# A batch's recurrence beside the whole next iteration, its feed-forward one iteration later, with three x buffers

## The chip, the cores and the metric

The program runs on one core of a Trainium2 chip. The metric is the device time of one execution in microseconds (us). Of the kernel before there are three timed executions: 1560.98, 1566.29 and 1566.89 us, median 1566.29. One more execution was profiled; it took 1569.24 us, of which 1567.4 us lie between the first and the last instruction (its span).

## What is computed

The reference is one decoder layer on x of 16 batches, 256 tokens and 512 channels, each of three parts followed by a residual and a layer norm:

```python
x = _layernorm(x + _L0_attn_ref(x, Wq, bq, Wk, bk, Wv, bv, Wo, bo))      # causal attention, 16 heads of 32
x = _layernorm(x + _L0_xattn_ref(16, 256, 512, time_decay, time_first, x, ctx_2048))
x = _layernorm(x + _L0_ffn_ref(x, W_gate, W_qkv))
```

The second part is a recurrence over the 256 tokens, per channel, with key x and value ctx:

```python
ww = u + kt;  q = max(pp, ww);  e1 = exp(pp - q);  e2 = exp(ww - q)
y_t = (e1 * aa + e2 * vt) / (e1 * bb + e2)
ww2 = pp + w; q2 = max(ww2, kt); e1b = exp(ww2 - q2); e2b = exp(kt - q2)
carry = (e1b * aa + e2b * vt, e1b * bb + e2b, q2)
```

The third part is again causal attention with 16 query heads, but with one key and one value head for all of them: a gate (softmax of x @ W_gate.T, then its argmax) picks for each token one of 16 key and value heads.

## The kernel before, in words

The 16 batches are independent. The names A, W and F stand for the three parts of a batch: first attention, recurrence, feed-forward attention. Every float32 matrix product is made of three f32r products (high x high, low x high, high x low), so that each operand is split once: ScalarE (ACT) writes the high part from PSUM, VectorE (DVE) the rest. In the code these are the functions ending in `_hi` and `_lo`.

Heads are handled in four groups of four. For a group, TensorE (PE) computes the scores twice. `sq` (three tiles) gives them with queries on partitions; DVE reduces each tile to a negated maximum (L1368); PE transposes those (`max_transpose`, L547); ACT and DVE split the row in two, `row_hi` and `rows` (L1373); two DMAs on SyncE (SP) write the rows into `q_stack`. Then `sk` (three tiles) computes the scores with keys on partitions, now with the maxima included; ACT takes the exponential (L1031); PE multiplies with the values (`values`), ACT copies, PE turns back (`turn`), DVE normalises. The operands `q_stack` and `k_stack` are built by DMAs out of `q_hi`, `q_lo`, `k_hi`, `k_lo` (`stack`, L322). In A, `out_transpose`, `out_hi` and `out_lo` prepare the output projection (jobs PA_WO and PA_WO + 1); `first_residual`, `first_stats` and `ln_apply` follow.

The recurrence works on the transposed x: `x1_transpose` brings a half (two blocks of 128 channels) into a PSUM bank. For each of the four blocks c DVE runs `recurrence_start` (a scan for the maxima and a difference), ACT five activations in `carry_exps` and one in `now_exps`, GpSimd (POOL) `weighted`, DVE `sums` (two scans), POOL `products`, DVE `divide` (a reciprocal), POOL `quotient`. `y_transpose` brings a half back, then `second_residual`, `second_stats`, `second_norm`. F starts with `x2_transpose`, projections on jobs PF_Q, PF_K, PF_V (two each), `gate_logits`, `gate_transpose`, `gating`, `pick_key`, `key_transpose`, `pick_value`, and then has the same four groups.

There is no scheduler. Each engine's order is written by hand, and semaphores join them. The steady part is `iteration(t)`: it runs A of batch t (from its last value projection on), F of batch t - 1, and at its end the first projections of batch t + 1 and the recurrence of batch t. The recurrence of t starts when A of t is through its layer norm and must end before F of t can start, early in the next iteration. `opening` runs batch 0 alone, `ending` the last recurrence and the last F. x of a batch stays in one of two buffers, `x_even` and `x_odd`. Eight PSUM banks exist: `pp` and `pw` for projections and transposes, `pt` for small transposes, two for `sq`, two for `sk`, `po`. All projections of the next batch go through `pp` from batch 2 on. Each engine works its list strictly in order: an instruction that waits holds all behind it.

## Time and profile before

| | us |
|---|---|
| median of three timed executions | 1566.29 |
| the profiled execution | 1569.24 |
| its span | 1567.4 |
| busy in the span: PE, DVE, ACT, POOL | 1419.3, 1124.4, 640.0, 412.3 |
| first and last x split for the next batch on ACT (L1102, 15 of them) | 61.7 and 1370.5 |

The profile gives the work of each engine over the span. PE is busy 91% of it, DVE 72%, ACT 41% and POOL 26%. In the chain of work that ended last PE holds 59% and DVE 26%. Busy time is a sum over parts of the program with different limits, so it has to be read by stretch. The ends of matmuls in the profile are modelled, since matmuls overlap; an idle time of PE is therefore shown shorter than the gap that it makes between the starts of two matmuls.

### The profile page before, as it was taken

The page shows a single profiled execution, that of the slowest core. Times are in us where ns is not written, and L with a number is a line of the kernel's source. Part 1 is how long each engine was busy: PE and PEld are TensorE (multiplying, and loading weights), DVE is VectorE, ACT ScalarE, POOL GpSimd, SP SyncE. Part 2 cuts the span into 40 slices and gives each one's busy share as a digit, 9 for nine tenths or more (in the row PEclk, how much of TensorE's full clock was granted, in tenths as well). Part 3 has the DMA queues.
Part 4 walks back from the last instruction along what each step waited for, and adds up shares of the span by engine and source line. Part 5 has one row for each costly group of instructions (what it writes and reads, how often), then busy time and mean ns, then how long its engine had stood idle before and what let it go on. Part 6 is the DMA issues. An engine that isn't in the chain of part 4 may idle for free.

```text
span 1567.4 us, 26626 instructions
## 1 busy us (share of the span) xinstructions
PE 1419.3 (91%) x9941; PEld 1123.7 (72%) x9941; DVE 1124.4 (72%) x2260; ACT 640.0 (41%) x1459; POOL 412.3 (26%) x550
## 2 busy tenths in 40 slices
PE   7879999899998989999899999989999998999886
PEld 6667777677777777777777777777777777777564
DVE  4475777868677686776868677786867768677774
ACT  3442533434344253433435344353434425353322
POOL 1350321414122141321414122141412214032130
PEclk9989999999999999999999999999999999999998
DMA  6432232333213233232333313233321323323110
GB/s 192 133 89 68 55 76 57 88 89 79 79 42 82 75 88 89 59 88 52 71 88 79 92 47 74 65 88 89 79 79 42 82 75 89 88 61 80 32 50 20
DMA packets 63199, 119.50 MB, mean 76 GB/s; under 512 B 14304, under 2 KB 32736, under 8 KB 63072
## 3 DMA queue, kind: packets, MB, share of 16 engines
q1 hardware_dynamic: 60400, 112.56, 28.6%
q10 hardware_dynamic: 2672, 5.24, 1.0%
q8 instruction: 80, 1.31, 0.4%
q14 instruction: 47, 0.39, 0.1%
HBM read 32.81 MB, written 8.39 MB: 26 GB/s over the span
## 4 chain that ended last, share of the span: by engine, by line
PE 59%; DVE 26%; ACT 7%; DMA 3%; issue 3%; SPq 1%; POOL 1%; DVEq 0%; ACTq 0%; POOLq 0%
PE pp L485 8%; PE pp L487 7%; PE pp L486 7%; PE po L590 7%; DVE neg_max L1368 5%; DVE w_key L1445 3%; PE po L594 3%; PE sq L531 3%; DVE w_max L1439 2%; PE sq L525 2%; PE pw L485 2%; PE pw L487 2%; PE pw L486 2%; PE sq L510 2%; DMA q_stack<-max_rows 2%
## 5 line engine op out<-in xcount | busy, mean ns | idle before, releaser
L1031 ACT ACTIVATE prob<-sk 128x512 f32<-128x512 f32 x384 | 215.0, 594 | 464.2 <-PE sk L510 463.7
L1368 DVE TENSOR_REDUCE neg_max<-sq 128x2 f32<-128x512 f32 (+1 forms) x384 | 249.7, 677 | 58.0 <-PE sq L510 54.9
L485 PE MATMUL pp<-xt_hi,w_hi 128*128 128x256 f32 x728 | 220.4, 303 | 20.8 <-DVE w_lo L1355 7.3
L487 PE MATMUL pp<-xt_hi,w_lo 128*128 128x256 f32 x728 | 206.3, 283 | 0.0
L486 PE MATMUL pp<-xt_lo,w_hi 128*128 128x256 f32 x728 | 206.3, 283 | 0.0
L485 PEld LDWEIGHTS pp<-xt_hi,w_hi 128*128 128x128 f32 x728 | 139.8, 192 | 32.9 <-issue 11.8
L486 PEld LDWEIGHTS pp<-xt_lo,w_hi 128*128 128x128 f32 x728 | 139.9, 192 | 0.7
L487 PEld LDWEIGHTS pp<-xt_hi,w_lo 128*128 128x128 f32 x728 | 139.6, 192 | 0.0
L1042 ACT ACTIVATE o_ch<-po 128x512 f32<-128x512 f32 x128 | 75.8, 592 | 136.2 <-PE po L594 136.2
L510 PE MATMUL sq<-mask_qk,ident_b 128*128 128x256 bf16 (+1 forms) x384 | 124.7, 325 | 0.0
L485 PE MATMUL pp<-w_hi,xt_hi 128*128 128x512 f32 x252 | 114.2, 453 | 10.7 <-DVE k_lo L1477 10.7
L510 PE MATMUL sk<-mask_kq,ident_b 128*128 128x256 bf16 (+1 forms) x384 | 123.4, 321 | 0.0
L1854 POOL TENSOR_TENSOR w_ev<-w_e,w_val 128x256 f32<-128x256 f32 x62 | 43.6, 704 | 260.8 <-ACT w_e L1089 229.0
L1445 DVE RECIPROCAL w_key<-w_key 128x256 f32<-128x256 f32 x62 | 107.5, 1734 | 0.0
L1820 POOL TENSOR_TENSOR var_eps<-meanvar,eps 128x2 f32<-128x2 f32 x48 | 9.3, 194 | 359.6 <-DVE meanvar L1404 359.6
L487 PE MATMUL pp<-w_hi,xt_lo 128*128 128x512 f32 x252 | 99.6, 395 | 0.0
L486 PE MATMUL pp<-w_lo,xt_hi 128*128 128x512 f32 x252 | 98.9, 392 | 0.0
L563 PE MATMUL sk<-q_stack,kf_stack 98*128 98x512 f32 x192 | 82.1, 467 | 6.9 <-DMA q_stack<-max_rows 3.3
L1373 DVE TENSOR_TENSOR max_rows<-pt,max_rows 8x128 fp32r<-8x128 f32 x128 | 35.3, 276 | 72.5 <-ACT max_rows L1064 70.0
L1839 POOL TENSOR_TENSOR xt_lo<-x_raw,xt_hi 128x1024 fp32r<-128x1024 f32 x15 | 35.6, 2373 | 189.9 <-ACT xt_hi L1102 189.9
L590 PE MATMUL po<-prob,v_f 128*33 128x256 f32 x512 | 80.0, 388 | 3.5 <-ACT prob L1031 2.3
L590 PE MATMUL po<-prob,v_a 128*33 128x256 f32 x512 | 80.7, 393 | 1.1 <-ACT prob L1031 1.1
(237 smaller groups left out, 3537.1 us busy)
## 6 DMA issues: line engine op xcount, KB each, us to landing
q_stack<-q_hi SPq DMA_DIRECT2D x256, 128.0 KB, 2.4
q_stack<-q_lo SPq DMA_DIRECT2D x128, 128.0 KB, 2.4
k_stack<-k_hi SPq DMA_DIRECT2D x128, 128.0 KB, 2.3
x_raw<-in_xT SPq DMA_DIRECT2D x16, 512.0 KB, 3.8
k_stack<-k_lo SPq DMA_DIRECT2D x64, 128.0 KB, 2.3
w_val<-in_ctxT SPq DMA_DIRECT2D x62, 128.0 KB, 2.2
w_raw<-in_weights ACTq DMA_DIRECT2D x4, 1024.0 KB, 6.5
q_stack<-max_rows SPq DMA_DIRECT2D x256, 4.0 KB
```

Of the source, the lines that this page charges most:

```text
L485: T.matmul(out, lh, rh, start=(c == 0), stop=False, skip_group_check=True)
L486: T.matmul(out, lh, rl, start=False, stop=False, skip_group_check=True)
L487: mm = T.matmul(out, ll, rh, start=False, stop=(c == CC - 1), skip_group_check=True)
L510: return T.matmul(out, ident_b[:], tile[:].unsqueeze(1).to_broadcast([P, heads, P]), start=False, stop=True, skip_group_check=True)
L531: T.matmul(out[:, S * k:S * (k + 1)], q_stack[0:3 * HD, h, P:S], key(h, 0, S, 3 * HD), start=(k == 0), stop=False, skip_group_check=True)
L563: T.matmul(out[:].rearrange("p (h q) -> p h q", h=heads), key(h, lo, P, rows), q_stack[0:rows, h:h + heads, q], start=True, stop=False, sk ...
L590: T.matmul(po[VW * j:VW * j + HD + 1, at:at + S], value(0, HG * g + k), prob0[:, k, :], start=True, stop=False, skip_group_check=True)
L594: mm = T.matmul(po[VW * j:VW * j + HD + 1, at + P:at + S], value(1, HG * g + k), prob1[:, k, :], start=False, stop=True, skip_group_check= ...
L1031: A.activation(dst, sk[n % 2][:], ACT.Exp, scale=SCALE).then_inc(s_exp, 1)
L1042: A.activation(o_ch[:].rearrange("p h q -> p (h q)"), po[:], ACT.Copy).then_inc(s_och, 1)
L1368: V.tensor_reduce(dst, src, AX.X, ALU.max, negate=True).then_inc(s_max, 1)
L1445: V.reciprocal(key, key).then_inc(w_rec, 1)
```

## The change

An iteration t now runs A of batch t, the second half of the recurrence of batch t - 1 (blocks 2 and 3), and F of batch t - 2; at its end stand the first half of the recurrence of batch t and the projections of t + 1. So three batches are under way, and x has three buffers. Iteration 1 has no F. `ending` has the rest of F of batch 13, all of F of batch 14, the last recurrence and F of batch 15. The overlays of recurrence buffers on `k_stack`, `k_hi` and `k_lo`, the second set of recurrence buffers for the last batch (`far`) and POOL's rewriting of the rows of ones in `k_stack` (`ones_back`) are gone. `picked` has a buffer of its own. The projections PA_K and PA_V of the next batch go to `pw`, so that Q, Q + 1, K, K + 1, V alternate as pp, pp, pw, pp, pw. The `keep` fillers of the ending are gone. All five engines' lists are rewritten.

```diff
-        k_stack, far_max, far_e2, far_d, far_e1, far_key, w_key, w_e1 = overlaid(
...
+        k_stack = sb("k_stack", [P, NH, S], f32r)
+        w_key = sb("w_key", [P, HC, S])
+        w_e1 = sb("w_e1", [P, HC, S])
...
-        x_even = sb("x_even", [P, TT, D])
-        x_odd = sb("x_odd", [P, TT, D])
+        x_bufs = [sb(f"x{i}", [P, TT, D]) for i in range(3)]
...
         def bank_of(b, job):
...
-            return pp
+            return pw if job in (PA_K, PA_V) else pp
...
+            def x1_transpose(b, half):
                 pe.wait_ge(x1_ready, b + 1)
+                wait(pe, w_free, W_JOBS * b + W_X1J + half)
+                if half == 1 and b == LAST:
+                    pe.wait_ge(u_free, U_JOBS * (b - 1) + U_X2 + 1)
+                elif half == 1 and b:
+                    pe.wait_ge(pa_free, PA_JOBS * (b + 1) + PA_V + 1)
+                turn_half(pw, x_of(b), half).then_inc(w_job, 1)
...
+            def x2_transpose(b):
                 pe.wait_ge(x2_ready, b + 1)
+                if b < LAST - 1:
+                    pe.wait_ge(w_free, W_JOBS * (b + 1) + W_X1J + 2)
...
-                        wait(pe, pf_free, PF_JOBS * b)
+                        wait(pe, pf_free, PF_JOBS * (b - 1))
...
                     elif job < PA_WO:
-                        wait(pe, pa_free, PA_JOBS * b + job)
+                        pe.wait_ge(pa_free, PA_JOBS * b + job - 1)
+                        if job == PA_K:
+                            pe.wait_ge(w_free, W_JOBS * (b - 1) + W_X1J + 1)
...
+            def iteration(t, last=False):
+                r, b = t - 1, t - 2
+                f = b >= 0
...
+                project_a(t, PA_V + 1, {1: lambda: sq_a(t, 0, 2), 2: first_max})
+                sq_a(t, 1, 0, 1)
+                if f:
+                    x2_transpose(b)
+                sq_a(t, 1, 2)
...
+                sk_a(t, 0, 0, 1)
+                max_a(t, 1)
+                sk_a(t, 0, 2)
...
+                if f:
+                    project_f(b, PF_V, fourth_turn)
...
+                    project_f(b, PF_V + 1, lambda: sq_f(b, 0, 2))
+                    max_f(b, 0, a_free, A_JOBS * a_done)
+                    sq_f(b, 1, 0, 1)
                 project_a(t, PA_WO)
...
             def iteration(t, last=False):          # on DVE
+                if t > 1:
+                    recurrence_start(r, 2)
+                maxima_a(t, 0, 2)
+                if t > 1:
+                    recurrence_start(r, 3)
+                rows_a(t, 0)
+                if b >= 1:
+                    last_third_residual(b - 1, x_of(b - 1))
+                maxima_a(t, 1, 0, 1)
+                if f:
+                    x2_split_lo(b, 0)
+                    x2_split_lo(b, 1)
                 maxima_a(t, 1, 2)
...
-            def ones_back(b):
...
             opening()
-            iteration(1, 1)
-            for t in range(2, NB - 1):
-                iteration(t, t % 2)
-            iteration(NB - 1, 1, True)
+            for t in range(1, NB):
+                iteration(t, t == LAST)
             ending()
```

How the change moves work is seen in two places. The first is DVE at the head of a steady iteration. Before, behind the first two maxima of group 0 of A (`neg_max`), there stand the sums of blocks 2 and 3 of the previous batch (L1437, L1439), its reciprocals (`w_key`) and its first residual (`x_odd<-pw`):

```order
L1368 TENSOR_REDUCE neg_max<-sq1 128x2
L1437 SCALAR_TENSOR_TENSOR w_e2<-w_e1_58,w_e2 128x256
L1439 SCALAR_TENSOR_TENSOR w_max<-w_e1_58,w_ev 128x256
L1368 TENSOR_REDUCE neg_max<-sq0 128x2
L1437 SCALAR_TENSOR_TENSOR w_e2<-w_e1_58,w_e2 128x256
L1439 SCALAR_TENSOR_TENSOR w_max<-w_e1_58,w_ev 128x256
L1373 TENSOR_TENSOR max_rows<-pt,max_rows 8x128
L1445 RECIPROCAL w_key_57<-w_key_57 128x256
L1368 TENSOR_REDUCE neg_max<-sq1 128x4
L1368 TENSOR_REDUCE neg_max<-sq0 128x2
L1445 RECIPROCAL w_key_57<-w_key_57 128x256
L1451 TENSOR_TENSOR x_odd<-pw,x_odd 128x2x256
```

Now the same place holds the starts of blocks 2 and 3 (L1552 to L1556) and the last residual of F of batch t - 3 (`x0<-x0,o_tok`):

```order
L1499 TENSOR_REDUCE neg_max<-sq1 128x2
L1552 SCALAR_TENSOR_TENSOR w_max<-decay,pw 128x256
L1554 MEMSET w_d 128x1
L1556 SCALAR_TENSOR_TENSOR w_d<-pw,decay,w_max 128x255
L1499 TENSOR_REDUCE neg_max<-sq0 128x2
L1552 SCALAR_TENSOR_TENSOR w_max<-decay,pw 128x256
L1554 MEMSET w_d 128x1
L1556 SCALAR_TENSOR_TENSOR w_d<-pw,decay,w_max 128x255
L1504 TENSOR_TENSOR max_rows<-pt,max_rows 8x128
L1523 RECIPROCAL o_rec<-po 128x8
L1524 TENSOR_TENSOR o_tok<-po,o_rec 128x256
L1687 TENSOR_TENSOR x0<-x0,o_tok 128x2x128
```

The sums and reciprocals of these blocks have moved down the list, behind the maxima of groups 1, 2 and 3.

The second place is PE ahead of the output projection of A (`w_hi,k_hi`). Before, score tiles of F's groups 0 and 1 and the values of group 0 stand between it and F's value projection:

```order
L563 MATMUL sk0<-q_stack,kf_stack_59 128x512
L510 MATMUL sk0<-mask_kq,ident_b 128x512
L531 MATMUL sq1<-kf_stack_59,q_stack 128x256 x2
L510 MATMUL sq1<-mask_qk,ident_b 128x2x128
L590 MATMUL po<-prob0,v_f 33x256 x2
L594 MATMUL po<-prob1_68,v_f 33x128 x2
L590 MATMUL po<-prob0,v_f 33x256 x2
L594 MATMUL po<-prob1_68,v_f 33x128 x2
L547 MATMUL pt<-ident,neg_max 8x128
L485 MATMUL pp<-w_hi,k_hi_63 128x512
```

Now the value projection (`pw<-w_hi,xt_hi`) is followed by one transpose and two score tiles:

```order
L467 MATMUL pw<-w_hi,xt_hi 128x512
L468 MATMUL pw<-w_lo_49,xt_hi 128x512
L469 MATMUL pw<-w_hi,xt_lo 128x512
L529 MATMUL pt<-ident,neg_max 8x128
L507 MATMUL sq1<-kf_stack_51,q_stack 128x128 x4
L492 MATMUL sq1<-mask_qk,ident_b 128x512
L513 MATMUL sq0<-kf_stack_51,q_stack 128x256 x2
L492 MATMUL sq0<-mask_qk,ident_b 128x2x128
L467 MATMUL pp<-w_hi,k_hi 128x512
```

The scores with keys on partitions and the values of group 0 have moved behind the output projection or into its second half.

## Rows read from the trace of the kernel before

**Rows 1.** Stretches: us, busy PE, PEld, DVE, ACT, POOL, PEclk, DMA share, GB/s.

```profile
0.00:96.40 96.40, 75.25 (x514) 62.37 (x514) 51.92 (x108) 43.77 (x98) 30.26 (x37) 0.96 0.56 159
96.40:200.30 103.90, 93.93 (x625) 74.53 (x625) 71.26 (x136) 41.00 (x95) 30.28 (x36) 0.92 0.25 62
200.30:1412.60 1212.30, 1125.70 (x7958) 892.82 (x7956) 898.89 (x1808) 505.00 (x1157) 320.49 (x430) 1.00 0.30 75
1412.60:1473.50 60.90, 56.55 (x387) 44.15 (x386) 41.84 (x86) 19.74 (x42) 10.45 (x17) 1.00 0.25 62
1473.50:1508.90 35.40, 24.64 (x183) 16.74 (x181) 31.52 (x61) 14.57 (x36) 18.39 (x24) 0.95 0.03 9
1508.90:1567.40 58.50, 43.18 (x282) 33.11 (x282) 29.00 (x66) 15.93 (x32) 2.47 (x8) 0.91 0.17 46
```

**Rows 2.** The same view, two stretches inside the iteration of batch 8.

```profile
756.00:773.00 17.00, 14.40 (x99) 10.95 (x97) 15.67 (x28) 7.69 (x18) 9.48 (x14) 1.00 0.45 101
773.00:790.00 17.00, 16.58 (x140) 14.22 (x141) 10.72 (x27) 7.10 (x15) 1.24 (x4) 1.00 0.10 34
```

**Rows 3.** What PE waited for, 251.5 to 1277.5 us, eleven iterations: total, times, longest.

```profile
PE pt L547 <- DVE neg_max L1368: 15.7, 22, 1.1
PE pp L485 <- DVE k_lo L1477: 13.1, 22, 0.7
PE pt L733 <- DVE k_lo L1490: 10.2, 9, 1.4
```

**Rows 4.** Timeline of PE at the K projections: start, length, [idle before].

```profile
745.70 0.27 PE L547 MATMUL pt<-ident,neg_max 128*8 128x128 f32 x1
746.45 0.38 PE L485 MATMUL pp<-xt_hi,w_hi 128*128 128x256 f32 x1 [0.47 <-DVE k_lo L1477]
751.42 0.50 PE L485 MATMUL pp<-w_hi,xt_hi 128*128 128x512 f32 x1 [0.69 <-DVE k_lo L1477]
```

**Rows 5.** Timeline of DVE, picking the value of one half.

```profile
804.80 0.67 DVE L1538 TENSOR_TENSOR w_val<-pp,g_ind 128x512 f32<-128x512 f32 x1
806.91 0.21 DVE L1392 RECIPROCAL o_rec<-po 128x8 f32<-128x8 f32 x1
```

**Rows 6.** Two lines of the program over the whole run: min/median/max ns.

```profile
L1545 DVE CAST k<-k_sel x32: 195/197/1334, 139.1 to 1526.7; 128x64 fp32r<-128x64 f32 x32
L1834 POOL TENSOR_TENSOR x_even<-x_even,bo_row x16: 1267/1287/1294, 53.1 to 1357.1; 128x512 f32<-128x512 f32 x16
```

**Rows 7.** Timeline of ACT, one carry_exps and the exponential behind it.

```profile
738.13 0.42 ACT L1084 ACTIVATE w_e<-w_d 128x256 f32<-128x256 f32 x1
739.91 1.06 ACT L1031 ACTIVATE prob<-sk 128x512 f32<-128x512 f32 x2
```

**Rows 8.** DVE's costliest lines of the recurrence: count, busy us, mean ns.

```profile
L1445 DVE RECIPROCAL w_key<-w_key 128x256 f32<-128x256 f32 x62 | 107.5, 1734 | 0.0
L1439 DVE TENSOR_TENSOR_SCAN w_max<-w_e,w_ev 128x256 f32<-128x256 f32 x62 | 62.3, 1005 | 0.0
```

**Rows 9.** Timeline of PE, maxima transposed and last turn: batches 0, 1 and the end.

```profile
31.03 0.27 PE L547 MATMUL pt<-ident,neg_max 128*8 128x128 f32 x1 [0.79 <-DVE neg_max L1368]
61.83 0.66 PE L604 MATMUL po<-ident,o_ch 128*128 128x128 f32 x4 [0.69 <-ACT o_ch L1042]
98.61 0.38 PE L547 MATMUL pt<-ident,neg_max 128*8 128x128 f32 x1 [0.79 <-DVE neg_max L1368]
1508.95 0.66 PE L620 MATMUL pw<-ident,x_odd 128*128 128x128 f32 x4 [1.50 <-DVE x_odd L1410]
1533.17 0.27 PE L547 MATMUL pt<-ident,neg_max 128*8 128x128 f32 x1
1557.90 0.66 PE L604 MATMUL po<-ident,o_ch 128*128 128x128 f32 x4 [0.69 <-ACT o_ch L1042]
```

**Rows 10.** Timeline of SP, stacking K; and its row of the page (KB, us to landing).

```profile
750.49 1.19 SPq L322 DMA_DIRECT2D k_stack<-k_hi  x2
k_stack<-k_lo SPq DMA_DIRECT2D x64, 128.0 KB, 2.3
```

More of the change, by code:

```diff
@@ L270, in bank_f @@
                 return po if job in (PF_Q + 1, PF_K + 1, PF_V + 1) else pp
+            if b == LAST - 1:
+                return pw if job == PF_K + 1 else pp
             return pw if job in (PF_K + 1, PF_V + 1) else pp
@@ L361, in k_stacks @@
                     wait(sp, pa_hi, 4 * b + PA_K + 2)
-                if groups[0] == NG - 1:
-                    wait(sp, w_ones, b + 1)
                 for g in groups:
@@ L376, in load_x @@
             def load_x(b, x):
-                if not (isinstance(b, int) and b < 2):
-                    sp.wait_ge(stored, 16 * (b - 1))
+                wait(sp, stored, 16 * (b - 2))
                 sp.dma_start(x[:], x_d[b].rearrange("(c p) d -> p c d", p=P)).then_inc(load_xa, 16)
@@ L715, in project_f @@
                 if bank is pw and job == PF_K + 1:
-                    pe.wait_ge(w_free, W_JOBS * (b + 1))
+                    pe.wait_ge(u_free, U_JOBS * (b + 1))
                 else:
-                    two = job > PF_Q if is_last(b) else job >= PF_V
+                    if bank is pw and job == PF_V + 1:
+                        pe.wait_ge(w_free, W_JOBS * (b + 2))
+                    two = job > PF_Q if is_last(b) else job == PF_V if b == LAST - 1 else job >= PF_V
                     pe.wait_ge(pf_free, PF_JOBS * b + (job - 1 if two else job))
@@ L724, in project_f @@
                 else:
-                    mm = tokens_out(bank, W_FV, job - PF_V, middle=middle, at=1)
+                    mm = tokens_out(bank, W_FV, job - PF_V, middle=middle)
                 mm.then_inc(pf_job, 1)
@@ L896, in value_a @@
+                sq_a(t + 1, 0, 0, 1)
+                x1_transpose(t, 1)
             def value_a(c, h):
@@ new lines, in ending @@
+                sq_f(b, 2, 2)
+                pe.wait_ge(dve_f, F_LINKS * b + F_LINK_PICKED + 1)
+                pe.wait_ge(f_norm, NG * b)
+                values_f(b, 0)
+                sk_f(b, 1, 0, 1)
+                turn_f(b, 0)
+                max_f(b, 2)
+                sq_f(b, 3, 0, 1)
+                sk_f(b, 1, 2)
+                sq_f(b, 3, 2)
+                values_f(b, 1)
+                y_transpose(LAST, 1)
+                sk_f(b, 2, 0, 1)
+                turn_f(b, 1)
+                max_f(b, 3)
@@ L970, in ending @@
+                sk_f(b, 2, 2)
+                values_f(b, 2)
+                sk_f(b, 3, 0, 1)
+                turn_f(b, 2)
+                sk_f(b, 3, 2)
+                x2_transpose(LAST)
                 values_f(b, 3)
-                keep(sq[0], 10)
-                y_transpose(LAST, 1)
+                project_f(LAST, PF_Q)
                 turn_f(b, 3)
-                keep(sq[0], 24)
                 b = LAST
-                x2_transpose(b, x_by_parity[b % 2])
-                keep(sq[0], 10)
@@ L1007, in _ @@
             opening()
-            iteration(1, 1)
-            for t in range(2, NB - 1):
-                iteration(t, t % 2)
-            iteration(NB - 1, 1, True)
+            for t in range(1, NB):
+                iteration(t, t == LAST)
             ending()
@@ L1339, in ending @@
                 copy_f(b, 3)
-                third_norm(b, x_by_parity[b % 2])
+                third_norm(b, x_of(b))
             opening()
-            iteration(1, 1)
-            for t in range(2, NB - 1):
-                iteration(t, t % 2)
-            iteration(NB - 1, 1, True)
+            for t in range(1, NB):
+                iteration(t, t == LAST)
             ending()
@@ new lines, in iteration @@
+                normalise_a(cha, t, 0)
+                maxima_a(t, 2, 2)
+                if t > 1:
+                    divide(r, 2)
+                out_lo(t, 0)
+                if f:
+                    gate_out(b)
+                rows_a(t, 2)
+                maxima_a(t, 3, 0, 1)
+                normalise_a(cha, t, 1)
+                if t > 1:
+                    divide(r, 3)
+                if f:
+                    fq_lo(b, 1)
+                maxima_a(t, 3, 2)
+                out_lo(t, 1)
@@ L1756, in ending @@
                 recurrence_start(LAST, 1)
+                maxima_f(b, 3, 0, 1)
+                third_residual(chf, b, 1, x_of(b))
+                x2_split_lo(r, 0)
+                x2_split_lo(r, 1)
+                sums(LAST, 0)
+                fq_lo(r, 0)
+                sums(LAST, 1)
+                maxima_f(b, 3, 2)
+                rows_f(b, 3)
+                divide(LAST, 0)
+                third_residual(chf, b, 2, x_of(b))
+                fq_lo(r, 1)
                 recurrence_start(LAST, 2)
```

900 lines of the change are left out of this document (504 added, 396 removed).

## The prediction

> **What bounds the kernel now.** I read busy time by stretch first [rows 1]. The middle, 200.3 to 1412.6 us, is 13 equal iterations: 1212.3 / 13 = 93.25 us each. PE is busy 1125.7 of it, 86.6 us per iteration, at a granted clock of 1.00, which is the level of 2.4 GHz. DVE has 69.1 us, ACT 38.8, POOL 24.7. So PE bounds the middle, and what can be won there is its 6.65 us of shown idle time per iteration, and a little more: at 745.70 and 746.45 [rows 4] the starts of two matmuls are 0.75 us apart where 0.47 are shown as idle, since the tail of the first overlaps the wait. I take 0.2 us for each of the 14 waits of an iteration (my reading of PE's timeline), 2.8 us. PE's work without waits is then 93.25 - 6.65 - 2.8 = 83.8 us.
>
> Next I read what PE waits for [rows 3]: maxima from DVE, the low parts of K from DVE, the key of F (`pt` L733). Nearly all of it comes from DVE, though DVE is idle a quarter of the time. The stretches tell why: from 756 to 773 us DVE is busy 15.67 of 17 us, from 773 to 790 only 10.72 of 17 [rows 2]; PE loses 2.6 us in the first and 0.4 in the second. In the first stretch the second half of the recurrence stands in DVE's list between the first maxima of the next batch, and F of that batch waits for its end. The end of the program shows the same chain alone: from 1473.5 to 1508.9 us PE is busy 24.6 of 35.4 us and DVE 31.5 [rows 1].
>
> **The change part by part.**
>
> *The steady iteration.* The instructions are the same but for `ones_back` on POOL, which no one on the path waits for, and three more interruptions of a projection by scores (14 against 11), which I price at 0.1 us each: 83.8 + 0.3 = 84.1 us without waits. Waits that go: the two before the K projections, 0.47 and 0.69 idle [rows 4], because K now has another bank than Q + 1 and V another than K + 1, and so need the low part of one job earlier; the one for the key of F, 10.2 us over nine iterations of eleven [rows 3], because PE now has a turn and `y_transpose` before it; the one before `x2_transpose`, because second_norm now ends most of an iteration earlier.
>
> Waits that come I worked out by laying the lists of all engines beside each other from the iteration's start, each piece at its start-to-start time in the timelines. Six places come out with PE first:
> - max_a(t, 0): DVE's `recurrence_start` of block 2 stands before the last tile of group 0. PE gets there at 1.9 us, the maximum at 2.3: 0.4.
> - max_a(t, 1): `x2_split_lo` twice stands before that maximum on DVE, and is itself behind ACT's carry_exps, 1.78 us [rows 7], and `x2_split_hi`. PE at 6.85, the maximum at 8.05: 1.2.
> - PA_WO: it needs the bank freed by `pick_value(b, 1)`. DVE has one pick (804.80 to 806.91, 2.11 us [rows 5]), a `rows` and a multiply before that, 3.0 us; PE has a transpose and two score tiles less than that. PE at 46.85, the bank at 48.05: 1.2.
> - the third `sk` tile of F's group 2, behind two carry_exps and `qk_hi` on ACT: PE at 70.9, ACT at 71.4: 0.5.
> - four other third `sk` tiles that follow the first two at once and need the first one's exponential: 0.35 each, 1.4.
> - the key: 0.4, below.
>
> Sum 5.1 us, period 84.1 + 5.1 = 89.2 us, against 93.25: 4.05 less. Lists laid out by hand find too few waits rather than too many. Bounds: below, half of them, 86.7; above, as many as before (9.45), 93.5. I stay at 89.2 because the three large ones can each be traced to one instruction, and DVE has 20 us free.
>
> The key is where GpSimd meets DVE. The copy L1545 takes 197 ns in the median and up to 1334, about the 1287 ns of POOL's add on x (L1834) [rows 6]. x of batch t is still loaded right behind the maxima of group 3, so the two adds fall on `pick_key(b, 1)` again. I take 0.4 us, between 0 and 2 x 1.1 us.
> The Trainium skill, "SBUF — State Buffer", section "SBUF: two separate sides", states that DVE and GpSimd share a port pair as an exclusive lock and that the loser blocks for the whole instruction. By that rule the wait stays whole and the sum would be up to 13 x 1.8 us higher; the maximum of L1545 agrees with it, its median says that it need not fall so. A rule, then, that speaks against part of the gain.
>
> The queue of SP issues a stack DMA every 0.6 us (two in 1.19 [rows 10]). The low part of K for group 0 is ready at 83.2 us, issued by 84.2, and PE wants it at 86.4. From issue to landing it takes 2.3 us [rows 10]. That is even to within half a microsecond; I price it at nothing, and at 0.5 us per iteration in the upper bound.
>
> *The opening and iteration 1.* Before, iteration 2 starts at 200.3 us. Now A of batch 1 runs without F. DVE ends the recurrence of batch 0 before the first maxima of batch 1, which puts the first transposed maximum at 102.5 us instead of 98.6 [rows 9]. From there four groups without cover take 61.83 - 31.03 = 30.8 us in batch 0, with weights still loading, and 1557.90 - 1533.17 = 24.7 in the last F [rows 9]; I take 26: 128.5. From batch 0's last turn (61.83) to the iteration behind it (96.4) are 34.6 us, of which I take off 4.6, since K and V have their own bank now: iteration 2 starts at 158.5. That is 41.8 us earlier, bounds 36 and 46.
>
> *The end.* From the start of iteration 15 to the output projection 60.9 us before [rows 1], 58 now. Then before: 35.4 us to `x2_transpose` of batch 15 at 1508.95 [rows 9]. Now there stand the rest of F of batch 13, all of F of batch 14 and the recurrence of batch 15. F alone takes from its `x2_transpose` to its last turn 1557.90 - 1508.95 = 49 us [rows 9], and F of batch 14 can start some 9 us into the stretch: 58 us if the recurrence hides wholly. DVE's list puts the recurrence's pieces between the maxima: two sums at 1.0 and 0.7 us, a reciprocal of 1.73 [rows 8] and a start of 1.1, four times, is 18 us; hidden not at all it gives 76. Walking through the lists I got 79 with waits. I take 74, near the upper end, because DVE holds both. 58 + 74 = 132 against 96.3: 35.7 longer, bounds 22 and 42. The last F: 58.5 before, 59.5 now, for the norm of batch 14 stands in it.
>
> So the two ends cost 158.5 + 132 + 59.5 = 350 us, against 355.1 before. F of one batch has moved from a place where A covers it to the end, and the opening has got shorter by the same.
>
> *The sum.* 350 + 13 x 89.2 = 1509.6 us of span. The profiled execution has 1.8 us outside its span and lies 0.2% over the median: 1511.4 x 1566.29 / 1569.24 = 1508.6, so 1509 us. The ends nearly cancel; each 0.1 us of the period is 1.3 us, and the break-even period is (1567.4 - 350) / 13 = 93.6 us.
>
> **Rivals.**
>
> *The clock falls in the thin stretches.* From 96.4 to 200.3 the granted clock was 0.92 and in the last F 0.91, where PE idles, against 1.00 in the middle [rows 1]. Now about 57 us of iteration 1 and 74 us of the end are thin, and the `keep` matmuls are gone. If PE runs at the 1.2 GHz level for a third of these 131 us, with 70% of it work, it loses 131 / 3 x 0.7 / 2 = 15 us: 1524. For it speaks that the clock did fall here; against it, that with waits on DVE PE's length seldom counts there.
> The Trainium skill, "TensorE: Matmul & The Clock Gate", section "Part 1: The HAM clock gate (the "warmup" mystery)", calls the throttled state the default, which activity releases; the rows agree with it in direction.
>
> *The waits come back elsewhere.* New hand-overs as tight as those removed hold the period at 92 to 93.3 us: 1546 to 1563 of span. For it speaks that every engine works in order and that the old list, too, left 9.45 us; against it, that DVE's crowded 17 us [rows 2] are now spread over a whole iteration.
>
> *Slower: DVE's queue at the head of the iteration.* There `recurrence_start` of blocks 2 and 3, 1.1 us each, the last residual of F, 1.07, and two `x2_split_lo`, 1.3, stand in front of the maxima of groups 0 and 1. If iteration after iteration DVE comes to this place late, because `divide(t, 1)` (1.73 us [rows 8]) and the low part of K end late, each of the four items is paid by PE in full: 4.6 us, which with my 5.1 makes 93.8, and with the 0.5 us for SP 94.3. It decides from 4.4 us on. Total 350 + 13 x 94.3 = 1576 of span. For it speaks the order of the list; against it, that I find DVE idle for 2 us just before.
>
> **How the numbers follow.** Forecast 0.62 (1485 to 1535); clock 0.11 (1515 to 1545); waits return 0.15 (1545 to 1563); slower 0.12 (over 1567). The range runs from 1476, the lower bound of the period (86.7, 33 us less), to 1556, which is the rival with returning waits for the most part, and leaves out the slower case. Within 0.5% of the median (1558 to 1574) is about what a measurement of this kernel can't tell from no change: 0.07, from the ends of the last two cases. Faster 0.80, slower 0.13.
>
> **What would show it.** The distance between x splits on ACT (L1102 before) should fall from 93.25 to about 89 us; in it PE's waits for the low part of K and for F's key are gone, and those for a maximum at the iteration's head and for the bank before PA_WO stand in their place. Iteration 2 should start near 158 us, and the last `x2_transpose` near 1450. The last F should be about 59 us long. I am wrong if the period is under 86 or over 92, or if the ends together lie 15 us off 350.

## The result, and the profile after

The changed kernel takes 1544.68 us (median of 4 runs, 1540.05 to 1548.85) against 1565.03 us; the ratio is 0.9886, 95% interval 0.9862 to 0.9910 (the two medians alone give 0.9870). It is faster by 1.1%, not by the 3.6% forecast: the direction was right, the size a third of what I said, and the time inside the range (1476 to 1556).

First the stretches of the profiled execution (1540.05 us, span 1538.2), with the columns of [rows 1]. Iteration 1, the 13 iterations of the middle, the last iteration up to the output projection, from there to the last `x2_transpose`, the last F. PEclk is the granted clock of PE: 1.00 is its 2.4 GHz level, 0.50 its 1.2 GHz level (the half clock).

```profile
96.40:171.50 75.10, 56.40 (x344) 43.63 (x343) 38.20 (x72) 24.18 (x53) 30.92 (x34) 0.85 0.20 52
171.50:1331.20 1159.70, 1107.08 (x7958) 886.85 (x7957) 868.25 (x1800) 509.76 (x1155) 302.38 (x399) 1.00 0.31 78
1331.20:1389.20 58.00, 54.77 (x380) 43.35 (x381) 43.37 (x93) 22.50 (x52) 12.80 (x18) 1.00 0.33 79
1389.20:1476.40 87.20, 63.28 (x380) 46.06 (x377) 57.86 (x119) 29.30 (x67) 17.83 (x28) 0.89 0.11 29
1476.40:1538.20 61.80, 45.32 (x293) 33.59 (x291) 30.36 (x71) 17.00 (x34) 2.48 (x8) 0.91 0.16 43
```

The reader sees two things. The middle is 1159.7 / 13 = 89.2 us per iteration at a clock of 1.00, and PE is busy 95% of it. The clock is 0.85 in iteration 1 and 0.89 behind the last output projection. Beside the forecast:

| us | before | forecast | after |
|---|---|---|---|
| iteration 2 starts | 200.3 | 158.5 | 171.5 |
| 13 iterations | 1212.3 | 1159.6 | 1159.7 |
| iteration 15 to last `x2_transpose` | 96.3 | 132 | 145.2 |
| last F | 58.5 | 59.5 | 61.8 |
| span | 1567.4 | 1509.6 | 1538.2 |

The middle came out to 0.1 us, which is closer than it repeats: in five traces below whose middle was not edited (warm1, open_order, tail, small_recip, warm_end) an iteration takes 89.3 to 89.5 us. The ends cost 378.5 us, not 350. The other runs of this kernel follow the clock: a mean of 0.980 goes with 1540.05 us, 0.973 with 1548.85. So the profiled run is the quickest of its kernel while that of before was slower than its median, and the traces differ by 29.2 us where the medians differ by 20.4.

What PE waited for in the middle (total, times, longest), as in [rows 3]:

```profile
PE pt L529 <- DVE neg_max L1499: 17.7, 25, 1.1
PE pp L467 <- DVE picked L1668: 15.2, 13, 1.2
PE sk L545 <- ACT prob L1128: 11.7, 39, 0.3
PE sk L550 <- DMA q_stack<-max_rows: 2.5, 4, 1.2
PE sk L545 <- DMA q_stack<-max_rows: 1.8, 5, 0.5
PE sq L507 <- DMA k_stack<-k_lo: 0.2, 1, 0.2
PE sk L555 <- ACT prob L1128: 0.2, 1, 0.2
```

The low part of K and the key of F are gone from the list. With 0.2 us for each wait beside its idle time, as in the forecast, this is (49.3 + 88 x 0.2) / 13 = 5.15 us per iteration, where 5.1 was forecast.

The place of the largest one, and the first maximum and last turn of batch 1, from PE's timeline (start, length, idle before):

```profile
754.91 0.50 PE L467 MATMUL pp<-w_hi,k_hi 128*128 128x512 f32 x1 [1.17 <-DVE picked L1668]
```

```profile
94.82 0.97 PE L507 MATMUL sq<-k_stack,q_stack 96*128 96x128 f32 x4 [3.18 <-DMA k_stack<-k_lo]
103.00 0.79 PE L513 MATMUL sq<-k_stack,q_stack 96*128 96x256 f32 x2 [4.05 <-DVE neg_max L1499]
105.11 0.41 PE L529 MATMUL pt<-ident,neg_max 128*8 128x128 f32 x1
139.02 0.65 PE L586 MATMUL po<-ident,o_ch 128*128 128x128 f32 x4 [0.69 <-ACT o_ch L1139]
```

The transpose at 105.11 takes 0.41 us, against 0.27 for the same one at 31.03 and 1533.17 [rows 9]. The stretches tell why:

```profile
95.00:105.10 10.10, 5.66 (x17) 3.75 (x17) 7.92 (x9) 4.29 (x10) 8.75 (x10) 0.50 0.09 20
105.10:139.00 33.90, 27.01 (x174) 19.89 (x172) 10.75 (x23) 11.73 (x24) 5.53 (x6) 0.80 0.23 64
139.00:171.50 32.50, 25.14 (x159) 21.28 (x160) 20.16 (x42) 9.54 (x23) 16.84 (x19) 1.00 0.22 53
```

The clock is at its 1.2 GHz level from 95 to 108.6 us, behind the 3.18 us wait for a DMA, and again from 125.7 to 135.9: 23.9 us. Between iteration 15 and the last `x2_transpose` it is there for 19.5 us, in five pieces. The ending holds these waits of PE, among others:

```profile
1428.61 0.50 PE L467 MATMUL pw<-w_hi,xt_hi 128*128 128x512 f32 x1 [4.06 <-DVE logit L1647]
1438.38 0.66 PE L507 MATMUL sq<-kf_stack,q_stack 96*128 96x128 f32 x4 [1.20 <-DVE kf_stack L1929]
1443.43 0.80 PE L513 MATMUL sq<-kf_stack,q_stack 96*128 96x256 f32 x2 [3.79 <-DVE neg_max L1499]
```

### The profile page after: what moved, and what is told of

Its sections match the earlier page's. It is cut to its first block, busy times and chain, and to the rows that moved or that the text cites. A ratio compares the mean times of both kernels' runs of the same rounds, so it can differ in the third digit from the quotient of the medians.

```text
span 1538.2 us, 26567 instructions
## 1 busy us (share of the span) xinstructions
PE 1403.6 (91%) x9858; PEld 1117.2 (73%) x9858; DVE 1088.6 (71%) x2258; ACT 647.1 (42%) x1459; POOL 391.6 (25%) x520
## 4 chain that ended last, share of the span: by engine, by line
PE 62%; DVE 13%; ACT 9%; issue 3%; SPq 2%; DMA 2%; POOL 0%; ACTq 0%; POOLq 0%; DVEq 0%
PE pp L467 7%; PE pp L469 6%; PE pp L468 6%; PE po L572 6%; PE pw L467 4%; PE pw L469 4%; PE pw L468 4%; DVE neg_max L1499 3%; PE po L586 3%; PE po L576 3%; PE sk L545 3%; PE sk L492 3%; ACT prob L1128 3%; PE sq L507 2%; PE sq L492 2%
## 5 line engine op out<-in xcount | busy, mean ns | idle before, releaser
L467 PE MATMUL pp<-xt_hi,w_hi 128*128 128x256 f32 x616 | 190.2, 309 | 12.7 <-DVE w_lo L1486 7.7
L468 PE MATMUL pp<-xt_lo,w_hi 128*128 128x256 f32 x616 | 175.2, 284 | 0.0
L469 PE MATMUL pp<-xt_hi,w_lo 128*128 128x256 f32 x616 | 175.2, 284 | 0.0
L469 PEld LDWEIGHTS pp<-xt_hi,w_lo 128*128 128x128 f32 x616 | 118.7, 193 | 0.0
L1523 DVE RECIPROCAL o_rec<-po 128x8 f32<-128x8 f32 x128 | 25.7, 201 | 112.2 <-PE po L586 110.9
L1161 ACT ACTIVATE max_rows<-pt 8x128 fp32r<-8x128 f32 x128 | 33.2, 259 | 163.8 <-PE pt L529 163.8
L467 PE MATMUL pp<-w_hi,xt_hi 128*128 128x512 f32 x200 | 89.7, 448 | 1.5 <-DVE k_lo L1607 1.1
L2043 POOL TENSOR_TENSOR w_y<-w_ev,w_key 128x256 f32<-128x256 f32 x64 | 46.9, 733 | 159.8 <-issue 119.0
L2007 POOL TENSOR_TENSOR x<-x,bo_row 128x512 f32<-128x512 f32 x32 | 40.3, 1282 | 185.2 <-DMA x<-in_x 185.2
L467 PE MATMUL pw<-w_hi,xt_hi 128*128 128x512 f32 x172 | 78.3, 455 | 4.5 <-DVE logit L1647 4.1
```

The costliest lines, as they stand in the source:

```text
L467: T.matmul(out, lh, rh, start=(c == 0), stop=False, skip_group_check=True)
L468: T.matmul(out, lh, rl, start=False, stop=False, skip_group_check=True)
L469: mm = T.matmul(out, ll, rh, start=False, stop=(c == CC - 1), skip_group_check=True)
L2043: G.tensor_tensor(w.y[:, i, :], w.ev[:, i, :], w.key[:, i, :], ALU.mult).then_inc(w_yr, 1)
```

## The experiments

Three theories stand beside each other for the 28.5 us at the ends: the clock; DVE's list, in which a step of the recurrence stands ahead of what PE waits for; and plain length that my estimate left out. Two more questions concern the middle: is the forecast right for the reasons it gives? All ratios are against the kernel before, with 95% intervals; the changed kernel's is 0.9886. It was not timed again beside them, and six edits at quite different places (warm1, open_order, wo_half, tail, small_recip, warm_end) all came out between 0.9824 and 0.9846. So a distance of 0.005 from 0.9886 can't be put down to one edit, and what an edit did is read from the stretches. These vary too where nothing was edited: iteration 2 starts at 169.5 to 176.1 us in the seven traces with the changed kernel's iteration 1, and the stretch from iteration 15 to the last `x2_transpose` takes 145.2 to 146.7 us in the three with its ending (the changed kernel, warm1, open_order). In the traces of the experiments the boundary before iteration 2 or 15 is set 2.3 us before the first transposed maximum of that batch, as it lies in the changed kernel.

**Fillers in iteration 1 (warm1).**

```
+                keep(sk[0], 24)
                 pe.wait_ge(a_max, TILES)
                 sq_a(1, 0, 0, 1)
...
+                def third_tile():
+                    fill(sk[0], 30)
+                    sq_a(t, 0, 2)
...
+                fill(pp, 6)
                 values_a(t, 1)
```

`fill` is `keep` in iteration 1 alone, and stands at eight places there: 30, 8, 6, 16, 12, 8, 10 and 6 matmuls.

> Filler matmuls (120, on banks free at that time) stand at ten waits of PE in iteration 1 and ahead of it; nothing else is changed. In the changed kernel batch 1's four groups take 33.9 us from the first maximum transposed (105.11) to the last turn (139.02), with a granted clock of 0.5 from 95.0 to 108.6 and from 125.7 to 135.9, where I had forecast 26 us. Clock theory: with the clock kept at 1.0 the four groups take 27 to 29 us and iteration 2 starts 5 to 8 us earlier, at 164 to 167 instead of 171.5. Rival, latencies (DMA landing, exponential, DVE's rows) set these groups whatever PE's clock: iteration 2 starts within 1.5 us of 171.5 or later by the fillers. Period 89.2 and the ending unchanged in both.

Measured 1539.66 us, 0.9846 (0.9815 to 0.9877). Stretches, as above:

```profile
96.40:166.30 69.90, 59.78 (x437) 47.49 (x438) 38.18 (x72) 23.70 (x52) 30.57 (x34) 1.00 0.21 55
166.30:1328.60 1162.30, 1108.48 (x7958) 887.43 (x7957) 869.11 (x1801) 510.19 (x1155) 302.97 (x399) 1.00 0.31 78
```

The clock is 1.00, and iteration 2 starts 5.2 us earlier, though the row holds 93 more matmuls. In the seven traces without an edit there it starts at 169.5 to 176.1, at clocks of 0.87 to 0.78, so 166.3 lies ahead of all of them.

**DVE's list in the opening (open_order).**

```
-                sums(0, 3)
-                divide(0, 2)
-                divide(0, 3)
                 maxima_a(1, 0, 0, 1)     # the three now follow in iteration(1)
```

> DVE does the first two maxima of batch 1 before the sums of block 3 and the reciprocals of blocks 2 and 3 of batch 0, which move into iteration 1 to the places that they have in later iterations. Queue theory: the first transposed maximum of batch 1 comes at about 100 to 101 instead of 105.1 and iteration 2 starts 4 us earlier, 167 to 168. Rival: the start of batch 1's groups isn't on the path of iteration 2 (its projections wait for something else): iteration 2 still starts at 171 to 172. By either the median falls by 0 to 5 us.

Measured 1538.48 us, 0.9835 (0.9807 to 0.9864):

```profile
96.40:166.60 70.20, 54.58 (x341) 42.98 (x342) 36.81 (x72) 24.22 (x53) 30.10 (x34) 0.91 0.24 59
```

Iteration 2 starts 4.9 us earlier, but the clock is 0.91 here, against 0.85. `plain_best` below has the same list at another clock.

**K and V again in the other projections' bank (kv_pp).**

```
-            return pw if job in (PA_K, PA_V) else pp
+            return pp
```

> One part of the change undone: from batch 2 on PA_K and PA_V go through bank pp again, so K waits for the low part of Q + 1, K + 1 for that of K, V for that of K + 1, V + 1 for value_out. In the kernel before these waits cost 0.74 + 0.93 + 0.50 us per iteration by start-to-start gaps. Theory that the bank swap carries about half of the period's gain: the period rises from 89.2 to 91 to 92.5, the median by 25 to 43 us. Rival, the waits are absorbed by other waits of the new order (sk tiles, head maxima): under 0.7 us per iteration, median under +10 us.

Measured 1616.69 us, 1.0335 (1.0305 to 1.0365). The middle, its waits, and one stretch in it:

```profile
PE pp L467 <- DVE k_lo L1607: 51.7, 26, 2.6
```

```profile
180.10:1406.90 1226.80, 1124.05 (x7958) 896.23 (x7957) 874.76 (x1800) 511.53 (x1155) 301.71 (x399) 0.99 0.30 74
734.20:737.60 3.40, 3.40 (x16) 2.79 (x15) 0.47 (x1) 1.19 (x2) 0.73 (x1) 0.50 0.00 0
```

The period is 94.4 us, above the kernel before. The waits for the low part of K come back at 51.7 / 26 = 2.0 us each, three times as long as before the change (13.1 / 22 = 0.6 [rows 3]). I had priced what the bank takes away at 1.6 us per iteration; here it is 5.2. The waits are 51.7 / 13 = 4.0 of it. PE's busy time is (1124.05 - 1107.08) / 13 = 1.3 us per iteration longer, and eight of the 13 iterations have a stretch at the half clock like the one shown.

**PA_WO waits for half of what it waited for (wo_half).**

```
-                        wait(pe, pf_free, PF_JOBS * (b - 1))
+                        wait(pe, pf_free, PF_JOBS * (b - 1) - 1)
+                    if job == PA_WO + 1:
+                        wait(pe, pf_free, PF_JOBS * (b - 1))
```

> PA_WO writes bank pp but waits until both value picks have read their banks, pp and pw. Here PA_WO waits for pp's alone and PA_WO + 1 for pw's. The wait ahead of PA_WO is 1.42 us per iteration in the changed kernel. If that is PE time, the period falls by 1.0 to 1.4 us to about 88.0 and the median by 13 to 18 us. Rival: the next hand-overs (the maxima of F's group 1, the rows of group 0, the exponentials) take it back: period 88.8 to 89.2, median within 5 us.

Measured 1537.83 us, 0.9830 (0.9802 to 0.9859). The waits of the middle:

```profile
PE pt L529 <- DVE neg_max L1501: 17.5, 24, 1.1
...
PE sq L513 <- DVE neg_max L1501: 10.6, 13, 0.8
```

The wait for the pick (15.2 us) is gone, and one for a maximum stands there instead (10.6 us). The period falls by 0.2 us only, no more than it differs between traces in which the middle was not edited.

**DVE's list in the ending (tail).**

```
-                sums(LAST, 2)
                 third_stats(b, x_of(b))
                 ...
                 gating(chf, r)
+                sums(LAST, 2)
...
+                maxima_f(r, 0)            # ahead of gate_value, second_residual
...
+                divide(LAST, 2)           # now behind maxima_f(r, 1) and (r, 2)
+                divide(LAST, 3)
```

> The ending only: in DVE's list the gating of batch 14 and its key stand ahead of the sums of block 2 of batch 15, the first maxima of F of batch 14 ahead of second_residual, and the last two divides of batch 15 behind the maxima of groups 1 and 2. In the changed kernel the ending (from the start of iteration 15 to the last x2_transpose) takes 145.2 us, forecast 132; PE waits 4.30 us there for the gating logit, 4.03 for the maximum of group 0 of F of batch 14. DVE-order theory: the ending is longer than forecast because DVE does a step of the recurrence ahead of what PE waits for; 5 to 8 us go, ending 137 to 140 us, ratio to the kernel before 0.984. Rival (the chain of batch 15's recurrence itself is the length, whatever stands first): the two waits go and come back behind the divides; ending 143 to 147 us, ratio as the changed kernel's 0.9886.

Measured 1538.12 us, 0.9824 (0.9798 to 0.9851).

```profile
1337.50:1479.02 141.52, 120.03 (x757) 90.20 (x756) 100.71 (x211) 51.97 (x119) 29.98 (x46) 0.92 0.20 50
```

```profile
1434.93 0.79 PE L467 MATMUL pw<-w_hi,xt_hi 128*128 128x512 f32 x1 [2.90 <-DVE logit L1647]
1445.05 0.50 PE L513 MATMUL sq<-kf_stack,q_stack 96*128 96x256 f32 x2 [0.50 <-DVE neg_max L1499]
1447.26 0.50 PE L467 MATMUL pp<-w_hi,xt_hi 128*128 128x512 f32 x1 [1.58 <-DVE picked L1668]
```

141.5 us against 145.2, between the two forecasts: 3.3 us of the 3.79 before the maximum go and half come back on the pick; of the 4.06 before PF_K + 1 only 1.2 go.

**A nearly free divide for the last batch (small_recip).** The reciprocals of batch 15's recurrence take one column, so most of that batch's normalisation is left out.

```
+                if is_last(b):
+                    key = key[:, 0:1]
                 V.reciprocal(key, key).then_inc(w_rec, 1)
```

> The reciprocals of the recurrence of batch 15 take one column in place of the whole key, which leaves out most of the normalisation of that batch; everything else is issued as before. Four reciprocals of 1.73 us lose some 1.6 us each, 6.5 us of DVE's work in the ending. If DVE's time in the ending is what PE waits for, the ending (145.2 us) gets 5 to 7 us shorter, ratio 0.984; if latency of the hand-overs between engines is, under 2 us.

Measured 1539.28 us, 0.9835 (0.9806 to 0.9863). The stretch takes 143.6 us, 1.6 less:

```profile
1336.30:1479.92 143.62, 119.83 (x757) 89.49 (x756) 95.10 (x211) 51.86 (x119) 30.64 (x46) 0.92 0.20 49
```

DVE has 6.1 us less to do (95.1 against 101.2), and three quarters of that bring nothing. The amount of this work on DVE is not what sets the length of the ending. The timed ratio, 0.005 below the changed kernel's, says nothing of this edit: five others have it too.

**Maxima first at the iteration's head (head).**

```
+                maxima_a(t, 0, 2)
                 if t > 1:
                     recurrence_start(r, 2)
-                maxima_a(t, 0, 2)
...
+                maxima_a(t, 1, 2)         # ahead of both x2_split_lo
```

> In DVE's list of every iteration the third maximum of group 0 stands ahead of recurrence_start of block 2, and the third maximum of group 1 ahead of the two x2_split_lo. The two waits of PE at the iteration's head (0.70 and 0.90 us per iteration in the changed kernel) should go. Queue theory (as in my forecast's walk through the lists: they are paid there and nowhere else): period 89.19 less 0.8 to 1.4, so 87.8 to 88.4, ratio 0.974 to 0.979. Rival (what the bank swap away from PA_WO showed: a wait removed is followed by another 1 us later): period 88.9 to 89.3, ratio within 0.003 of the changed kernel's.

Measured 1551.36 us, 0.9908 (0.9881 to 0.9936).

```profile
175.80:1344.50 1168.70, 1119.17 (x7954) 888.03 (x7953) 876.77 (x1798) 509.76 (x1155) 305.12 (x399) 1.00 0.31 77
```

```profile
PE pp L602 <- ACT v_a L1216: 5.5, 13, 0.4
PE sq L513 <- DVE neg_max L1499: 5.0, 12, 0.4
```

The waits for a transposed maximum (17.7 us before this edit) are gone, these two stand in their place, and the period is 89.9 us, 0.7 longer. The theory that these waits are paid there and nowhere else is false: taking them away did not shorten the period. Why it grew is open. The listed waits do not say it: PE's shown idle time is even less (1168.7 - 1119.2 = 49.5 us, against 1159.7 - 1107.1 = 52.6), while its busy time is 12.1 us longer with the same matmuls at a clock of 1.00. That what DVE now does later is itself needed soon after is likely, but not shown.

**The pick behind the maxima, with and without the relaxed wait (wo2, pick_late).**

```
-                    pick_value(chf, b, 1)
-                    assert chf.n == F_LINK_PICKED + 1
                     maxima_f(b, 1, 0, 1)
+                    pick_value(chf, b, 1)
+                    assert chf.n == F_LINK_PICKED + 1
```

> As wo_half (PA_WO waits for the first pick of F's second group only), and besides DVE takes the first two maxima of group 1 ahead of pick_value(b, 1). wo_half had lost the 1.42 us wait before PA_WO but had 0.97 us on a maximum of F's group 1 in its place (period 88.99). If that maximum is late because the pick stands before it: both go, period 88.0 to 88.3, ratio 0.974 to 0.977. Rival (DVE's whole load around there): period 88.8 to 89.2.

> Only DVE's order: the first two maxima of F's group 1 ahead of pick_value(b, 1), and the wait of PA_WO as in the changed kernel. With the wait relaxed as well (wo2) the period is 87.82 against 89.19. Two-place theory (the pick stands in front of both PE's bank and PE's maximum, and each edit alone only moves the wait): the wait before PA_WO grows by the two maxima, 1.2 us, to 2.6; period 89.8 to 90.4, ratio 0.994 to 1.003. Rival (the whole gain of wo2 was the order of the maxima): period 88.0 to 88.4, ratio 0.974.

wo2: 1520.03 us, 0.9718 (0.9688 to 0.9748). pick_late: 1575.42 us, 1.0077 (1.0055 to 1.0099). The middle of wo2:

```profile
169.50:1311.50 1142.00, 1104.76 (x7956) 887.42 (x7955) 864.89 (x1799) 509.87 (x1155) 302.83 (x399) 1.00 0.32 79
```

Of pick_late, what PE waited for in the middle, one such wait in the timeline, then a stretch behind it and the whole middle:

```profile
PE pp L467 <- DVE picked L1668: 30.8, 13, 2.4
```

```profile
495.68 0.50 PE L467 MATMUL pp<-w_hi,k_hi 128*128 128x512 f32 x1 [2.37 <-DVE picked L1668]
```

```profile
496.70:500.10 3.40, 3.40 (x9) 2.67 (x8) 0.31 (x2) 0.00 (x0) 0.00 (x0) 0.50 0.03 7
171.30:1361.30 1190.00, 1120.58 (x7957) 897.18 (x7957) 862.43 (x1799) 509.75 (x1155) 301.71 (x399) 0.99 0.30 76
```

The same edit of DVE's list wins 1.2 us per iteration when PE's wait is relaxed (87.8 against 89.0 for wo_half) and loses 2.3 when it is not (91.5 against 89.2). The two places are one. The loss is larger than the 1.2 us by which the wait grew (a period of 89.8 to 90.4 had been expected): behind the 2.37 us wait PE goes on at the half clock, and of the 13 iterations eight have such a stretch. PE's busy time is (1120.58 - 1107.08) / 13 = 1.0 us per iteration longer, which with the 1.2 makes 2.2 of the 2.3. `kv_pp`, with waits of up to 2.6 us, has eight such stretches too.

**Fillers in the ending (warm_end).**

```
+                keep(pw, 12)              # before max_f(b, 3)
+                keep(sk[0], 16)           # behind turn_f(b - 1, 3)
+                keep(sk[0], 16)           # before sq_f(b, 0, 2)
+                keep(sk[0], 8)            # before sq_f(b, 1, 2)
+                keep(pp, 14)              # before values_f(b, 2)
```

> The changed kernel with 66 keep matmuls of 512 columns at five places of the ending where PE waits (1.5 to 4.3 us each); nothing reads them. In the changed kernel the clock is at its half level for 20.4 us of the 76 before the last x2_transpose. Clock theory: these stretches cost the ending about what the two of iteration 1 did (5.2 us for 23.9 us): ending 4 to 5 us shorter than 145.2, ratio 0.9855. Rival (the ending is a chain of hand-overs over DVE and ACT, on which PE's length hardly counts, or the fillers themselves come late): within 1.5 us of 145.2, or longer.

Measured 1539.23 us, 0.9841 (0.9818 to 0.9865).

```profile
1332.40:1471.78 139.38, 120.57 (x823) 91.89 (x822) 100.98 (x211) 51.70 (x119) 30.63 (x46) 0.98 0.20 51
1471.78:1531.60 59.82, 43.25 (x293) 31.99 (x291) 30.60 (x71) 16.89 (x34) 2.48 (x8) 0.94 0.17 45
```

```profile
1443.58 0.50 PE L513 MATMUL sq<-kf_stack,q_stack 96*128 96x256 f32 x2 [0.41 <-DVE neg_max L1506]
```

The stretch is 5.8 us shorter, a little more than the clock theory said. The last F, which holds no fillers, is 2.0 us shorter; but it is 59.9 us in small_recip too, so this can't be put down to the fillers. The pair of score matmuls that took 0.80 us at 1443.43 takes 0.50.

**Together (plain_best, best).** plain_best is wo2, open_order and tail; best adds the fillers of warm1 and warm_end.

> wo2, open_order and tail together, no fillers. Their differences from the changed kernel's ratio (0.9886) are -0.0168, -0.0051 and -0.0062. If the three places are independent, the ratio is 0.9605 and the time 1504; if the opening's and the ending's parts were mostly the drift of the clock from run to run, 0.966 to 0.970.

> plain_best with the fillers of warm1 in iteration 1 and of warm_end in the ending. If the clock costs time beside the order of the list (clock theory): 5 us less than plain_best from iteration 1 and up to 4 from the ending, ratio 0.955. Rival: once DVE's order is mended PE idles less there, the clock falls less, and both gains overlap: within 0.002 of plain_best.

plain_best: 1516.48 us, 0.9700 (0.9680 to 0.9719). best: 1510.25 us, 0.9663 (0.9643 to 0.9684). Stretches of plain_best:

```profile
96.40:172.40 76.00, 60.24 (x344) 46.56 (x344) 37.99 (x73) 24.48 (x53) 30.25 (x34) 0.81 0.22 55
1314.70:1452.97 138.27, 115.69 (x756) 87.19 (x756) 100.63 (x211) 52.08 (x119) 29.98 (x46) 0.95 0.21 51
```

and of best:

```profile
96.40:167.00 70.60, 60.32 (x441) 48.01 (x441) 37.47 (x73) 25.21 (x56) 30.55 (x34) 1.00 0.22 57
167.00:1310.10 1143.10, 1105.10 (x7958) 887.71 (x7957) 860.77 (x1800) 509.74 (x1155) 302.52 (x399) 1.00 0.32 79
1310.10:1447.15 137.05, 119.01 (x823) 90.58 (x822) 100.34 (x211) 51.73 (x119) 29.96 (x46) 0.99 0.21 52
1447.15:1507.00 59.85, 43.26 (x293) 31.98 (x291) 30.62 (x71) 16.88 (x34) 2.48 (x8) 0.94 0.17 45
```

The parts do not add up to 0.9605. For the opening, set the start of iteration 2 in all traces beside the clock from 96.4 us to there:

| iteration 1 | trace: iteration 2 starts (clock) |
|---|---|
| as in the changed kernel | wo2 169.5 (0.87), warm_end 171.1 (0.85), pick_late 171.3 (0.86), changed kernel 171.5 (0.85), wo_half 172.0 (0.85), small_recip 173.1 (0.86), tail 176.1 (0.78) |
| with fillers | warm1 166.3 (1.00) |
| DVE's list mended | open_order 166.6 (0.91), plain_best 172.4 (0.81) |
| both | best 167.0 (1.00) |

(kv_pp and head are left out, since their edits touch iteration 1.) In the first row nothing there was edited, and by and large iteration 2 starts the later the lower the clock. At a clock of 1.00 the mended list brings nothing (167.0 against 166.3). At a clock near 0.8 it may: 172.4 against 176.1 in tail, one trace each. So most of open_order's 4.9 us need not be the list's; how much is, these traces do not settle.

In the ending the list alone was worth 3.7 us. best is 2.3 us below the fillers alone (137.05 against 139.38), but 1.4 of these come from the relaxed wait: PA_WO starts 47.6 us into iteration 15 there, 49.0 in warm_end and in the changed kernel. Beside the fillers the list is worth 0.9 us. best beats both kernels: 3.4% faster than before.

## Why the prediction was right in direction and wrong in size

The step that failed is "the two ends cost 350 us, against 355.1 before", by which the ends cancel. They cost 378.5, which takes 23.4 of the 52.6 us that the middle gains. Both terms left their own bounds: iteration 2 came 28.8 us earlier (36 to 46), the stretch to the last `x2_transpose` got 48.9 us longer (22 to 42). The sign of being wrong that I had named, ends 15 us off 350, is met: they are 28.5 off. In place of that step the runs showed 11.0 us of half clock, a cost that the sum had put at nothing; lengths mis-sized by 7.8 us in iteration 1 and 7.4 behind the last output projection; and 2.3 us in the last F. Each of these is read from one trace or two, and iteration 1 alone varies by up to 6.6 us between traces in which nothing there was edited, so the shares are rough. The period, the stretch up to the output projection and the last F held to within 2.3 us each.

*What bounds the kernel, and the period.* Right: 89.2 forecast, 89.2 measured, and in the main for the reasons given. DVE's maxima at the head, 0.4 + 1.2 forecast, cost (17.7 + 25 x 0.2) / 13 = 1.75 us; PA_WO 1.2, measured 1.4; the third `sk` tiles 1.9, measured 1.5. A wait for the DMA of the maxima's rows, 0.5, was not foreseen, and the key cost nothing instead of 0.4. That it fits to 0.1 us is partly luck: I had counted 14 waits of 0.2 us per iteration of the kernel before, while the profile lists 111 in eleven iterations, 10 each, and by that count the forecast would have been 90.0. On the key I had said that POOL's adds fall on the key's copy again. They no longer do: 12 of the 32 copies took over 0.4 us before, 2 take it now.

```profile
L1675 DVE CAST k<-k_sel x32: 194/195/1283, 206.1 to 1497.4; 128x64 fp32r<-128x64 f32 x32
```

The median is nearly the same, the maximum (1283 ns, POOL's add 1283 ns in the median) still that of an add. The rule in the Trainium skill, "SBUF — State Buffer", section "SBUF: two separate sides", that VectorE and GpSimd take a shared port pair as an exclusive lock, fits what a collision costs; that it speaks against part of the gain did not come true, since most of the collisions went.

*What the bank is worth.* My two waits of 0.47 and 0.69 [rows 4] understate it: 5.2 us per iteration in the new order, 1.3 of them more busy time of PE. The forecast did not need this price, because it came from the lists laid out anew and not from the old waits.

*Iteration 1: 158.5 forecast, 171.5 measured, 13.0 off.* First maximum 102.5 against 105.1, then 26 against 33.9 for the four groups, then 30 against 32.5. The clock is 5.2 of it (warm1; 4.5 between the changed kernel and best). With the clock at 1.00 and the forecast's own list, the three are 104.0, 29.9 and 32.4 (warm1); with the list mended 103.8, 30.8 and 32.4 (best). So the four groups cost near what they cost batch 0, 30.8 us [rows 9], which I had in hand and lowered to 26 by the last F; that the two figures are so close is partly chance, since the clock was 0.89 in batch 0's. It is a term that was mis-sized, by 3.9 us in warm1; the other two are 3.9 together.

*The end: 132 forecast, 145.2 measured, 13.2 off.* Up to the output projection 58 forecast, 58.0 measured. Behind it 74 against 87.2. The clock is 5.8 of it: with the forecast's own lists and a clock of 0.98, 139.4 - 58 = 81.4 us are left (warm_end). Of the 7.4 us above my 74, 5 are a term mis-sized: walking through the lists I had got 79, and I set it down to 74 without a reason from a row. The other 2.4 the walk missed. DVE's order is worth 3.7 us alone and 0.9 beside the fillers, so it is no third cause of like size. "If the recurrence hides wholly, 58" was no real bound either. It let F of batch 14 start at its `x2_transpose`, while groups 2 and 3 of F of batch 13 still stand between on PE: in PE's timeline the `x2_transpose` of batch 14, the last turn of batch 13, the first maximum of batch 14, and for comparison both for the last F:

```profile
1397.80 0.41 PE L602 MATMUL pw<-ident,x 128*128 128x128 f32 x2 [0.53 <-DVE w_d L1556]
1423.95 0.60 PE L586 MATMUL po<-ident,o_ch 128*128 128x128 f32 x4
1448.11 0.27 PE L529 MATMUL pt<-ident,neg_max 128*8 128x128 f32 x1
1476.41 0.63 PE L602 MATMUL pw<-ident,x 128*128 128x128 f32 x2
1505.36 0.27 PE L529 MATMUL pt<-ident,neg_max 128*8 128x128 f32 x1
```

Batch 14 needs 50.3 us from its `x2_transpose` to its first maximum, batch 15 needs 29.0, and 26.2 of the 50.3 are gone before the last turn of batch 13.

*The last F:* 59.5 forecast, 61.8 measured at a clock of 0.91, 59.8 in warm_end at 0.94.

*The rivals.* The first, the clock, is what happened for some two fifths of the miss. I gave it 15 us and a chance of 0.11, at a third of 131 us at the half clock; there were 23.9 + 19.5 = 43.4 us of it, a third, and the fillers bring back 5.2 + 5.8 = 11.0 of the 28.5 us. Up to another 2.0 are in the last F, where nothing separates the clock from chance. What spoke against it, that PE's length seldom counts beside waits on DVE, was wrong. The change had itself taken 83 `keep` matmuls, which are such fillers, out of the ending. The clock should have been a term of the sum: the clock of [rows 1] was already 0.92 and 0.91 in the stretches that were to grow thinner. The page "TensorE: Matmul & The Clock Gate" of the Trainium skill, section "Part 1: The HAM clock gate (the "warmup" mystery)", states that activity releases the throttled state; the fillers, which are activity and nothing else, agree with it: the clock of iteration 1 rose from 0.85 to 1.00. Waits that return (0.15) is false for the changed kernel and true of a neighbour: in wo_half the removed wait came back within the iteration. In head, too, two waits went and the period did not fall, but the listed waits do not account for its length. The slower case, DVE's queue at the head, did not occur: 1.75 us of its 4.6 were paid.

## What to carry to other kernels

When work is moved out of a thin place into a full one, the thin place that is left behind needs a sum of its own, with the clock as a term of it; read its length from the most similar stretch, not from a shorter one. A number that comes from walking through the lists is not rounded toward a bound. When an engine's list and another engine's wait speak of the same buffer, change both or neither: the order alone (pick_late) lost 2.3 us per iteration, the wait alone (wo_half) won 0.2, which is within the differences between traces, both together (wo2) won 1.4.

## What the runs showed of the hardware that I had not expected

Waits of 2.37 us (pick_late) and 2.6 us (kv_pp), one in each iteration of an otherwise full middle, had the granted clock at the 1.2 GHz level behind them in 8 of 13 iterations; in the other five the same wait had no such stretch behind it. Where PE's waits in the middle were at most 1.2 us, there was none (the changed kernel) or one in 13 iterations (wo_half, open_order, small_recip). A long wait is then paid twice: pick_late's grew by 1.2 us and its period by 2.3.

The clock is not the same in every execution of the same instructions: with nothing edited there, iteration 1 had 0.78 to 0.87 in seven traces, and iteration 2 started up to 6.6 us apart.
